# A four-layer convolution kernel in which TensorE's products signal less often

## What is computed

```
# layer 0: mixture of 8 experts on 2x2 patches (128 values a token, 256 tokens an image)
for e in range(E):
    h = xp @ w1[e]
    val, g = jnp.split(h, 2, axis=-1)
    he = val * jax.nn.sigmoid(g)
    out = out + gate[:, e:e + 1] * (he @ w2[e])
# layer 1: deformable 3x3 convolution; every pixel gathers 9 taps x 4 corners
sampled = gather_corner(y0, x0, ...) + gather_corner(y0, x0 + 1, ...) + ...
out = jnp.einsum('bckhw,ock->bohw', sampled, w.reshape(CO, C, K2))
# layer 2: state-space convolution over 1024 positions, then a gated unit
y = jax.nn.gelu(jnp.swapaxes(y, 1, 2))
g = y @ W_glu + b_glu
g = g[..., :D_MODEL] * jax.nn.sigmoid(g[..., D_MODEL:])
h = _layernorm(h + g, ln_gamma, ln_beta)
# layer 3: depthwise 7x7 convolution, layernorm, two small products with gelu
```

## Time and profile before

| | us |
|---|---|
| time, median of 3 runs | 1706.59 (1701.79 to 1708.61) |
| profiled execution: its own time, which is its span (the page shows nothing around it) | 2212.2 |
| POOL busy / PE busy / DVE busy / ACT busy in it | 1208.5 / 1480.2 / 981.2 / 547.5 |
| PE instructions that raise a semaphore | 1012 products |
| mean granted clock of TensorE | 0.81 of 2.4 GHz |

### The profile page before, as it was taken

One profiled execution on the slowest core, in us unless ns is written; L12 is line 12 of the kernel. 1 busy time (PEld: TensorE's weight loads), 2 busy tenths in 40 slices (PEclk: granted clock), 3 DMA queues, 4 the chain that ended last, 5 costly groups with the idle time before them and its releaser, 6 DMA issues.

```text
span 2212.2 us, 14137 instructions
## 1 busy us (share of the span) xinstructions
PE 1480.2 (67%) x4202; PEld 653.9 (30%) x4202; DVE 981.2 (44%) x1645; ACT 547.5 (25%) x874; POOL 1208.5 (55%) x1418
## 2 busy tenths in 40 slices
PE   7636651899645865957847765867847743665797
PEld 6432221343312322322313322322312311222245
DVE  3423342444422347842523247842431393323585
ACT  1111110233211231232322231231221302222446
POOL 8645455456465546566546546566546475565230
PEclk9867875899767887978967877978967985778899
DMA  6211221231212112321212112321212111211100
GB/s 198 56 52 49 55 55 51 69 91 51 60 46 75 47 37 60 82 58 43 68 33 77 51 37 59 82 59 43 59 40 56 29 50 40 64 42 49 31 8 13
DMA packets 111883, 123.08 MB, mean 56 GB/s; under 512 B 50880, under 2 KB 88896, under 8 KB 111424
## 3 DMA queue, kind: packets, MB, share of 16 engines
q0 software_dynamic: 36864, 75.57, 12.6%
q1 hardware_dynamic: 73888, 43.14, 7.6%
q10 hardware_dynamic: 1056, 3.47, 0.4%
HBM read 99.79 MB, written 9.01 MB: 49 GB/s over the span
## 4 chain that ended last, share of the span: by engine, by line
PE 33%; another core or an unknown queue 26%; DVE 17%; issue 15%; ACT 7%; DMA 1%; SPq 1%; DVEq 0%; ACTq 0%
PE bank L1960 6%; PE bank L1973 5%; DVE rb L1733 4%; PE bank L1875 4%; PE bank L1885 3%; PE bank L1867 3%; DVE gt L1617 3%; PE bank L1910 3%; PE bank L1943 2%; PE bank L1996 2%; DVE he L1515 1%; PE bank L1982 1%; DVE gt L1619 1%; DVE bst L1440 1%
## 5 line engine op out<-in xcount | busy, mean ns | idle before, releaser
L1137 POOL DMA_INDIRECT gt<-corner_table,idx x1152 | 1135.0, 985 | 877.1 <-DVE sm L1625 493.7
L1973 PE MATMUL bank<-yg,wts 128*128 128x512 f32 x512 | 252.2, 636 | 56.5 <-issue 30.9
L1960 PE MATMUL bank<-u,wk 128*128 128x512 f32 x512 | 254.0, 642 | 14.2 <-ACT yg L1298 4.0
L1659 DVE SCALAR_TENSOR_TENSOR tg<-tg,ae 128x512 f32<-128x512 f32 x64 | 44.4, 694 | 403.6 <-ACT ae L1310 342.0
L1875 PE MATMUL bank<-xg,w_sb 128*128 128x512 f32 (+1 forms) x288 | 156.1, 626 | 68.4 <-issue 38.9
L1515 DVE SCALAR_TENSOR_TENSOR he<-he,bank 128x512 f32<-128x512 f32 (+1 forms) x144 | 89.9, 626 | 206.0 <-remote 83.0
L1885 PE MATMUL bank<-he,w_sb 128*128 128x512 f32 (+1 forms) x288 | 150.1, 606 | 35.3 <-DVE he L1515 26.8
L1617 DVE TENSOR_TENSOR gt<-gt,bank 128x1152 f32<-128x1152 f32 x128 | 172.5, 1347 | 1.1
L1867 PE MATMUL bank<-xp,w_sb 128*128 128x512 f32 (+1 forms) x288 | 151.5, 610 | 20.3 <-ACT he L1212 13.6
L1212 ACT ACTIVATE he<-bank 128x512 f32<-128x512 f32 (+1 forms) x144 | 79.1, 549 | 307.6 <-PE bank L1867 157.3
L1733 DVE SCALAR_TENSOR_TENSOR rb<-xp,par,rb 128x1024 f32<-128x1024 f32 x124 | 155.1, 1292 | 0.0
(11 more groups left out here) (249 smaller groups left out, 1557.3 us busy)
## 6 DMA issues: line engine op xcount, KB each, us to landing
gt<-corner_table,idx POOLq DMA_INDIRECT x1152
tb<-gate_of_token SPq DMA_DIRECT2D x56, 256.0 KB
u<-sqb SPq DMA_DIRECT2D x48, 128.0 KB
corner_table<-tb SPq DMA_DIRECT2D x36, 128.0 KB, 2.9
w_sb<-w ACTq DMA_DIRECT2D x2, 1024.0 KB, 6.8
xp<-xg SPq DMA_DIRECT2D x56, 32.0 KB
X<-x SPq DMA_DIRECT2D x1, 1536.0 KB, 10.9
out<-X SPq DMA_DIRECT2D x6, 256.0 KB
```

The lines of the kernel that those rows point to most:

```text
L1137: pool.indirect_dma_start(gt[:, t % GRING, k].rearrange("p a c -> p (a c)"), None, corners, bass.IndirectOffsetOnAxis(ap=idx[s % 2][:, j, ...
L1960: op = mm(psum[b][:, :], wk[:, t, d], u4[:, g, at:at + HALF], start=t == 0, stop=t == JJ - 1 and n > 0)
L1973: op = mm(psum[B2.bank(*name)][:, :], w_glu[:, k, col + d * P:col + (d + 1) * P], yg[:, c % 2, k], start=k == 0, stop=k == NB2 - 1)
```

## The change

Three products lose their semaphore increment, and whoever waited for one of them waits for a later product of the same order on PE: "gate" is now told by "value", "gb" by "ga", and "z" of d = 0 by "z" of d = 1. A fourth semaphore, `he_used`, goes altogether: ACT's tanh of a unit now waits for that unit's "value", which PE makes after the out product that `he_used` told of. `Banks` counts only the products that still signal. The products, their order, the banks and the order table are the same. The programs built from the two texts have 1012 and 637 products of PE with an increment (144 "gate", 135 out, 64 "gb" and 32 "z" fewer), and ACT has 129 separate wait instructions fewer.

```diff
+def signalled_by(kind, *k):
+
+    if kind == "gate":
+        return ("value", *k)
+    if kind == "gb":
+        return ("ga", *k)
+    if kind == "z":
+        return ("z", *k[:2], NB2 - 1)
+    return (kind, *k)
+
 class Banks:
     def __init__(self, full, free, plan):
         self.full, self.free = full, free
-        self.where, count = {}, {}
+        self.where, self.told, count, signals = {}, {}, {}, {}
         for name, bank in plan:
             self.where[name] = (bank, count.get(bank, 0))
             count[bank] = count.get(bank, 0) + 1
+            if signalled_by(*name) == name:
+                signals[bank] = signals.get(bank, 0) + 1
+                self.told[name] = (bank, signals[bank])
...
     def filled(self, eng, *name):
-        b, k = self.where[name]
-        eng.wait_ge(self.full[b], FROM + k + 1)
+
+        b, k = self.told[signalled_by(*name)]
+        eng.wait_ge(self.full[b], FROM + k)
...
                 B0.filled(act, "gate", a, u)
                 if u == PAIR + 1:
                     B0.filled(act, "out", a, 0)
-                elif u >= 2:
-                    act.wait_ge(S["he_used"], used(a, u - 2))
...
-                mm(psum[b][:, 0:w], w1_sb[:, e, 2 + h], tokens(xpf, images), start=True, stop=True).then_inc(full[b], 1)
+                mm(psum[b][:, 0:w], w1_sb[:, e, 2 + h], tokens(xpf, images), start=True, stop=True)
...
-                mm(psum[2][:, 0:w], w2_sb[:, e, h], he[:, u % 2, 0:w], start=first, stop=last)\
-                    .then_inc(full[2] if last else S["he_used"], 1)
+                op = mm(psum[2][:, 0:w], w2_sb[:, e, h], he[:, u % 2, 0:w], start=first, stop=last)
+                if last:
+                    op.then_inc(full[2], 1)
...
                     for k in range(NB2):
                         op = mm(psum[B2.bank(*name)][:, :], w_glu[:, k, col + d * P:col + (d + 1) * P],
                                 yg[:, c % 2, k], start=k == 0, stop=k == NB2 - 1)
-                    op.then_inc(full[B2.bank(*name)], 1)
+                op.then_inc(full[B2.bank("ga", s, c, d)], 1)
...
-                mm(psum[b][:, :], wenc[r, d * P:(d + 1) * P], u4[r, g, at:at + HALF], start=True, stop=True)\
-                    .then_inc(full[b], 1)
+                op = mm(psum[b][:, :], wenc[r, d * P:(d + 1) * P], u4[r, g, at:at + HALF], start=True, stop=True)
+                if d == NB2 - 1:
+                    op.then_inc(full[b], 1)
```

More of the change, by code:

```diff
@@ L83, in place_in @@
     return images.index(g) if len(images) > 1 else m % 2
-def used(a, u):
-    return sum(len(units(i)) // PAIR * (PAIR - 1) for i in range(a)) + u // PAIR * (PAIR - 1) + u % PAIR + 1
 def pieces(a):
@@ L777, in build @@
             var_ready0 var_ready1 var_ready2 var_ready3 std_ready0 std_ready1 std_ready2 std_ready3
-            xn0_ready xp_in o_in max_ready exp_ready gate_ready gate_out patch_ready he_used
+            xn0_ready xp_in o_in max_ready exp_ready gate_ready gate_out patch_ready
             xpad_ready rows_ready om_ready mask_ready idx_ready smp_ready relu_done
```

## The result

| | before | after |
|---|---|---|
| time, median (lowest to highest) | 1705.49 us (1701.79 to 1708.61, 4 runs) | 1724.34 us (1722.84 to 1725.34, 4 runs) |
| ratio, 95% interval | | 1.011 (1.0092 to 1.0128) |

The change made the kernel 18.9 us slower, 1.1%, against the 1711 us that I held likeliest: inside the range, on the side of the second rival. The first thing to read is the busy time of each engine, then the gathers, in the changed kernel's profile.

What follows compares the result with a forecast made beforehand. The prediction took POOL's gathers to bound the timed kernel; 2.9 us (first image) + 0.7 ("gb") + 0.7 ("z") made 4.3 us on top of 1706.6, so 1711 us, with a range of 1684 to 1730.

Steps and rivals of the forecast that it cites:

- the second rival: Layer 0's 512-column pairs and gated units: later tanh isn't covered; 1731 us at half price, 1750 in full; chance 0.31.
- What bounds the kernel: Timed kernel: POOL's gathers bound it, 1636 to 1688 us without stalls, leaving 19 to 71 us for POOL's stalls.
- the profiled execution's 505.6 us: Whole kernel: timed runs need 505.6 us less than the profiled 2212.2, nearly all late increments, little present when timed.
- Its fall with the number of increments: Profiled execution: 37% fewer increments take 211 of 571 us of late increments away, giving 2005 us.
- The third rival: PE: increments cost time one by one; a gain of 9 us or more needs 24 ns each; chance 0.02.
- the first: Timed runs have late increments too, so fewer shorten the line: 7 to 26 us saved, 1685 to 1704; chance 0.24.
- First image: Before the first gather: tanh waits for "value", 0.36 us a pair, 8 pairs, 2.9 us slower.
- Units of 512 columns: Layer 0's 56 pairs: later tanh could cost 0.42 us each; likeliest 0, upper end 23.5 us.
- the ring's 45 us of gathers: Against the second rival: POOL's ring of four tiles holds some 45 us of gathers, letting PE and DVE catch up.
- Gated units: Tanh of "gb" waits for "ga": 16 us at most, likeliest 0 until gathers end, 0.7 us in the last image.
- "z": Last image: first "z" reading waits for the second product, second reading ends about 0.7 us later; elsewhere nothing moves.
- The signs: Changed kernel's profile: value releases tanh, first gather near 78 us, span near 2005; wrong if over 26 us faster.

Runs made afterwards that it cites:

- second profile: The kernel before, unchanged, timed and profiled once more: 1704.67 us, ratio 0.9999 (0.9988 to 1.001).

## Why the prediction was right and wrong

- **What bounds the kernel: right.** The gathers, 997 ns with 0.30 between them, are 58% of the second profile's chain, and a start 2 us later moved the end by 2.2 us at least. Between 295 and 440 us, though, POOL waits for DVE's `sm`, and most of the loss was made there. Setting the profiled execution's 505.6 us aside as its own was right too.
- **Its fall with the number of increments: wrong.** Against the profile the sum was 2005 us. The span is 1722.1 because late increments did not come again, with 637, 1012 or 1692 increments alike.
- **Increments cost nothing by themselves: right.** This was read from equal passes; the removal of 135 and the addition of 680 show it in the time. The third rival fell, and so did the first: there was no line of increments to shorten.
- **First image: right.** Its 2.9 us were 3.8, with 2.9 inside the interval (2.2 to 5.5); a pair grew by 0.44 instead of 0.36 us.
- **Units of 512 columns: the step that failed.** It reads "I take 0 for the likeliest case and 23.5 us as the upper end". The measured term is 8.4 us. The price of a pair was near, 0.42 against 0.52 us. It is paid in 16 of 56 pairs, those between 295 and 410 us, where PE is full. The reason for the 0 was that PE was full only because "it catches up after late increments". The second profile has none, and PE is busy for 110.31 of 115 us there. The row that I dismissed was right: 460 to 515 us of the first profile is the second half of this very pass, and its last six scaled inputs lie in 38.7 us that the second profile repeats in every busy time and count. The first profile, then the second:

```profile
466.90:505.60 38.70, 38.70 (x97) 17.03 (x95) 16.25 (x26) 9.70 (x16) 19.32 (x21) 1.00 0.23 61
```

```profile
355.40:394.10 38.70, 38.70 (x97) 17.03 (x95) 16.25 (x26) 9.70 (x16) 19.32 (x21) 1.00 0.22 61
```

So PE was not catching up there; that work fills it in both profiles. What I held against the rival, that the ring's 45 us of gathers let PE catch up, fails with it. POOL already waited 16.3 us for `sm` in that stretch before the change, from 370 us on, so the ring was used up, and what PE lost there came on top:

```profile
POOL gt L1137 <- DVE sm L1625: 16.3, 3, 7.1
```

- **Gated units: failed too, and the cause is open.** "Likeliest 0 until the gathers end" and 0.7 us in the last image, with 16 us in full; measured 4.8 us (2.4 to 7.3). Behind the gathers it is 1.4 us (111.24 instead of 109.81), which kernels with an unchanged last image reach as well. For the other 3.4 us, I can name the wait of "z" for its bank, 5.7 us in total, but POOL's wait for `sm` grows by 2.6 us only, and no run shows in which images it counts.
- **"z": right in place, small in size.** 0.7 became 2.2 us (0.3 to 3.9); the last image's timeline has 1.45, because a piece of layer 3 stands between the two readings.
- **The second rival, slower,** had mechanism and place right. Half its price gave 1731; measured is 1724.3. The forecast of 1711 was 13 us short, and its range held the result only because it took in half of this rival's price. With the terms as measured, 11.6 + 4.8 + 2.2 on 1705.5, the sum is 1724.1.
- **The signs.** Tanh is released by the value product, and the first gather starts at 77.79 us, as forecast (near 78). PE idle ahead of the value products in 512 columns, with POOL waiting for `sm` behind them, was named as what would prove the forecast wrong, and is what the waits show.

## What to carry to other kernels

A signal that a later product implies is free to remove if its reader does not become later for it: `he_used` went at no cost. "Gate", "gb" and "z" made a reader wait for the product behind. For "gate" the runs show where that is paid: 0.52 us a pair where the engines had no gap, and nothing that can be told in the other 40 pairs of 512 columns. Such a delay costs by what is queued behind the delayed instruction; moving one independent DVE operation ahead of it took back all 11.6 us, and gave 3.2 us without the change. Where a profile is far longer than the timed runs, take a second one before deciding which of its rows are its own: here the stretch without a gap, which I set aside, was in both.

## What was not expected of the hardware

One profiled execution of thirteen, the first of the kernel before, had 571 us of its chain under "another core or an unknown queue", which I read as increments that reached their readers late, and took 2212.2 us; the same program profiled again took 1703.9. The gathers took as long in both, 985 and 997 ns. The first one's trace also holds fewer semaphore updates, 11138 against 28224, so what it says of who released a wait rests on incomplete records. The number of increments isn't the cause; what is stays open.
